# Inverse denominators spread through memory and second-norm statistics on ScalarE, in a fused attention and expert kernel

## What is computed

```
h = layernorm(x) * (1 + ca) + sa
x = x + ga * attention(h)          # 16 heads of 16 channels
h = layernorm(x) * (1 + cb) + sb
x = x + gb * experts(h)            # 1 shared, 8 routed, the best 2 weigh
# attention: q, k scaled and clipped; Tq, Tk Chebyshev orders 1..5
num = sum_n Tq[n] * beta[n] * cumsum(Tk[n] * v)
den = sum_n sum_d(Tq[n]) * beta[n] * cumsum(sum_d(Tk[n]))
out = num / (den + 1e-7)           # den is one number per head and token
# layernorm: (x - mean) / sqrt(var + 1e-5) over the 256 channels
```

## Time and profile before

| what | us |
|---|---|
| median of 3 runs | 1037.01 |
| lowest, highest | 1036.67, 1037.52 |
| the profiled execution | 1036.65 |
| its span in the trace | 1034.9 |

### The profile page before, as it was taken

The page is one execution under the profiler, slowest core; times in us unless marked ns, Lnnn a source line. Parts: engine busy times, 40 slices in busy tenths (PEclk is TensorE's granted clock), DMA queues, the critical chain, the costliest instruction groups (busy, mean ns, idle before and its releaser), DMA issues. The chain is left out here.

```text
span 1034.9 us, 15465 instructions
## 1 busy us (share of the span) xinstructions
PE 935.0 (90%) x4889; PEld 674.1 (65%) x4889; DVE 890.0 (86%) x1385; ACT 475.8 (46%) x702; POOL 399.9 (39%) x631
## 2 busy tenths in 40 slices
PE   3965659999999999999999999999999999989995
PEld 3643346685767676776857676776758676757774
DVE  2488989999999999999999999999999999998431
ACT  4343345553536455554635454455535364431431
POOL 2022454443625244443625253443535152443210
PEclk9977889999999999999999999999999999999998
DMA  8103222223323132223332231232332231312111
GB/s 283 47 1 61 61 41 64 49 63 61 71 45 79 21 63 70 41 61 61 72 61 61 40 69 44 41 73 49 72 61 41 41 72 22 67 36 46 42 21 20
DMA packets 38428, 59.34 MB, mean 57 GB/s; under 512 B 2067, under 2 KB 31198, under 8 KB 38374
## 3 DMA queue, kind: packets, MB, share of 16 engines
q0 software_dynamic: 15360, 33.56, 19.0%
q1 hardware_dynamic: 21410, 22.72, 6.7%
q10 hardware_dynamic: 1604, 2.46, 0.7%
HBM read 16.77 MB, written 16.79 MB: 32 GB/s over the span
## 5 line engine op out<-in xcount | busy, mean ns | idle before, releaser
L797 ACT ACTIVATE hid<-ring,b1row 128x512 f32<-128x512 f32 x144 | 98.6, 685 | 177.5 <-PE ring L1279 177.5
L639 POOL DMA_DIRECT2D feat<-feat x48 | 45.7, 952 | 334.3 <-DVE feat L984 150.3
L1416 PE MATMUL acc<-w,hid 128*128 128x256 f32 x640 | 156.4, 391 | 0.0
L1416 PEld LDWEIGHTS acc<-w,hid 128*128 128x128 f32 x640 | 115.3, 189 | 30.0 <-issue 14.5
L1111 DVE TENSOR_TENSOR hid<-hid,cfb 128x512 f32<-128x512 f32 x128 | 86.3, 674 | 41.8 <-PE cfb L1390 41.1
L752 ACT ACTIVATE feat<-ring,bqkv 128x512 f32<-128x512 f32 x96 | 66.1, 689 | 109.0 <-PE ring L1279 109.0
L963 DVE TENSOR_TENSOR_SCAN feat<-zero,carry,feat 128x512 f32<-128x512 f32 x80 | 111.8, 1446 | 0.0
L963 DVE TENSOR_TENSOR_SCAN feat<-zero,feat 128x512 f32<-128x512 f32 x80 | 108.5, 1403 | 0.0
L1279 PE MATMUL ring<-n2H,w1H 128*128 128x512 f32 x288 | 99.9, 428 | 0.0
L1279 PE MATMUL ring<-n2H,w1L 128*128 128x512 f32 x288 | 91.0, 397 | 0.0
L1279 PE MATMUL ring<-n2L,w1H 128*128 128x512 f32 x288 | 90.6, 395 | 0.0
(11 more groups left out here) (167 smaller groups left out, 2013.9 us busy)
## 6 DMA issues: line engine op xcount, KB each, us to landing
feat<-feat POOLq DMA_DIRECT2D x48, 512.0 KB, 4.6
xin<-in_L_attn_x SPq DMA_DIRECT2D x16, 512.0 KB, 5.4
out<-x SPq DMA_DIRECT2D x16, 512.0 KB, 4.5
out<-fin POOLq DMA_DIRECT2D x16, 512.0 KB, 6.1
gates<-gate_rows SPq DMA_DIRECT2D x16, 128.0 KB, 4.7
feat<-in_L_wmod SPq DMA_DIRECT2D x1, 1536.0 KB, 14.1
feat<-in_L_attn_W_in SPq DMA_DIRECT2D x1, 768.0 KB, 9.5
const<-in_constants ACTq DMA_DIRECT2D x1, 690.5 KB, 4.1
```

Of the source, the lines that this page charges most:

```text
L639: g.dma_start(f(into), f(of), accum_op=ALU.add).then_inc(added[n], 16)
L797: a.activation(hid[:, e % NG], ring[bank][:, :], ACT.Silu, bias=b1row[:, e:e + 1]).then_inc(ring_copied, 1)
L1416: last = mm(acc[t // 2][:, t % 2], x[:, t * P:(t + 1) * P], w[:, e // 2], start=False, stop=(e == E), skip_group_check=True)
```

## The change

The denominators are laid out anew: eight products accumulate in one PSUM tile of 128 rows (head times 8 plus block of 64 tokens) by 64 columns, so `invert` works on 128x64. `spread_inverse` leaves TensorE; SP writes the inverses to device memory and reads them back with each head's row repeated for its 16 channels, into the buffer `attn`, and `divide` multiplies in place. The selection matrix `headsel` is gone from the constants.

The second norm's statistics leave VectorE. ScalarE sums each token's channels (`token_sums`), GpSimd makes the negated mean (`token_means`), ScalarE sums the squared differences (`token_squares`, in two halves), and GpSimd makes scale and shift in four instructions (`inv_std_of_squares`). The passes stand between the copies of the projections; `scale_even` moves behind `normalise_second`. SP's loop is unrolled. VectorE's product for order 3 also waits for the squares, since their output is scratch in its buffer.

```diff
-        denom = sb("denom", [P, 2, P])
+        denom = sb("denom", [P, 2, TB])          # TB = 64, NB = 8
+        inv_rows = nc.dram_tensor("inv_rows", [H, CT], f32).ap()
+        squared = feat[:, W + 2].rearrange("p h (a d) -> p (h a) d", a=NT // KD)
...
+        def token_sums(act, i, p):
+            c = number(i, p)
+            for t in range(NT):
+                act.wait_ge(x1_ready, 2 * c + 1 + t // 2)
+                last = nc.scalar.activation(squared[:, t], x1[:, p, t], ACT.Copy, accum_out=ms[:, 1, 0, t:t + 1])
+            last.then_inc(sums_ready, 1)
+        def token_means(pool, i, p):
+            pool.wait_ge(sums_ready, number(i, p) + 1)
+            nc.gpsimd.tensor_tensor(ms[:, 1, 1], ms[:, 1, 0], k_("-1/D", NT), ALU.mult).then_inc(mean_ready, 1)
+        def token_squares(act, i, p, half):
+            act.wait_ge(mean_ready, number(i, p) + 1)
+            for t in (2 * half, 2 * half + 1):
+                last = nc.scalar.activation(squared[:, t], x1[:, p, t], ACT.Square, bias=ms[:, 1, 1, t:t + 1],
+                                            accum_out=ms[:, 1, 2, t:t + 1])
+            last.then_inc(squares_ready, 1)
+        def inv_std_of_squares(pool, i, p):
+            pool.wait_ge(squares_ready, 2 * c + 2)
+            # mult by 1/D; add eps; pow -half; mult by the negated mean, each behind the one before
...
 # SP
+            def spread_inverse(i, p):
+                c = number(i, p)
+                sp.wait_ge(den_inv, c + 1)
+                sp.dma_start(inv_rows.rearrange("h (b t) -> (h b) t", b=NB), denom[:, 1]).then_inc(inv_written, 16)
+                sp.wait_ge(added[0], 16 * (c + 1))
+                sp.wait_ge(inv_written, 16 * (c + 1))
+                for k in range(KD):
+                    rows = inv_rows[k * HPH:(k + 1) * HPH].unsqueeze(1).to_broadcast([HPH, DH, CT])
+                    sp.dma_start(attn[:, k], rows).then_inc(inv_spread, 16)
                 if loads or i < B:
+                    spread_inverse(i, p)
                     store_x1(i, p)
-            with sp.Fori(2, B - 2) as i:
+            for i in range(2, B - 2):
...
 # GpSimd
-                    inv_std(pool, 1, *later(i, p, -1))
+                    token_means(pool, *later(i, p, -1))
+                    inv_std_of_squares(pool, *later(i, p, -1))
...
 # ScalarE
                     highs(0, *nxt)
+                if second:
+                    token_sums(act, *prev)
                 silu(2)
-                if attn_:
-                    scale_even(i, p)
-                for half in HALVES[:4]:
-                    copy(half)
+                copy("k0")
+                if second:
+                    token_squares(act, *prev, 0)
+                copy("k1")
+                if second:
+                    token_squares(act, *prev, 1)
+                copy("q0")
+                copy("q1")
                 if second:
                     normalise_second(act, *prev)
+                if attn_:
+                    scale_even(i, p)
                 silu(3)
...
 # VectorE
                     dve.wait_ge(odd_ready, 4 * c + 1)
+                    ge(dve, squares_ready, 2 * c)
...
-                v.tensor_scalar(denom[:, 0], misc[:, 0:P], EPS_DEN, None, ALU.add).then_inc(den_eps, 1)
+                v.tensor_scalar(denom[:, 0], misc[:, 0:TB], EPS_DEN, None, ALU.add).then_inc(den_eps, 1)
...
+                dve.wait_ge(inv_spread, 32 * (c + 1))
                 for k in range(KD):
-                    dve.wait_ge(inv_spread, 2 * c + k + 1)
-                    v.tensor_tensor(attn[:, k], feat[:, W, k], tr[k][:, :], ALU.mult).then_inc(attn_ready, 1)
+                    v.tensor_tensor(attn[:, k], feat[:, W, k], attn[:, k], ALU.mult).then_inc(attn_ready, 1)
...
                     residual(*prev)
-                    token_stats(dve, 1, *prev)
...
 # TensorE
-                for t in range(NT):
-                    last = mm(misc[t * QS:(t + 1) * QS, 0:P], cv["densum"],
-                              prod[:, t * P:(t + 1) * P], start=True, stop=True)
+                for b in range(NB):
+                    last = mm(misc[:, 0:TB], cv["densum"][:, b * P:(b + 1) * P],
+                              prod[:, b * TB:(b + 1) * TB], start=(b == 0), stop=(b == NB - 1))
...
                 expert(5)
-                if attn_:
-                    spread_inverse(i, p)
                 expert(6)
```

More of the change, by code:

```diff
@@ L27 @@
 LQ = 2 * QS
+NB = P // H
+TB = CT // NB
 XS = 4
@@ L54 @@
 ROWS = head_rows()
-CONSTS = {"ident": P, "headsum": 4 * QS, "densum": QS, "headsel": NT * KD * P, "kshift": 1, "rowmask": 2,
+CONSTS = {"ident": P, "headsum": 4 * QS, "densum": NB * P, "kshift": 1, "rowmask": 2,
           "biases": 2, "tie": E * E, "cfsel": E * P}
@@ L71, in constants @@
             w = GAMMA[n] if n in (0, 2, 4) else 1.0
-            for copy in range(QS // H):
-                c["densum"][row, copy * H + half * HPH + h] = w
+            for b in range(NB):
+                c["densum"][row, b * P + (half * HPH + h) * NB + b] = w
             c["kshift"][row, 0] = {1: -0.5 * DH, 3: -0.125 * DH}.get(n, 0.0)
-    for q in range(4):
-        for half in range(KD):
-            c["headsel"][q * QS + half * HPH + ch // DH, (q * KD + half) * P + ch] = 1.0
     c["rowmask"][:SPL // 2, 0] = 1.0
@@ L113, in build @@
         tie = cv["tie"].unsqueeze(1).to_broadcast([P, NT, E * E])
-        PC = ("-half", "half", "one", "eps", "1/D", "e")
+        PC = ("-half", "half", "one", "eps", "1/D", "-1/D", "e")
         pool_c = sb("pool_c", [P, len(PC)])
@@ L227, in build @@
         rstd_ready = [sem(f"rstd{n}_ready") for n in range(2)]
+        sums_ready, mean_ready = sem("token_sums"), sem("token_means")
+        squares_ready, var_steps = sem("token_squares"), sem("token_variance_steps")
         norm_ready = [sem(f"normalised{n}") for n in range(2)]
@@ L247, in build @@
         den_ready, den_eps, den_inv = sem("denominators"), sem("denominators_eps"), sem("denominators_inverse")
-        inv_spread = sem("inverse_spread")
+        inv_written, inv_spread = sem("inverse_written"), sem("inverse_spread")
         attn_ready = sem("attention_ready")
@@ L376, in token_stats @@
             last.then_inc(stats_ready[n], 1)
+        def token_sums(act, i, p):
[15 more added lines that the diff above has]
+            c = number(i, p)
+            at = 3 * c
+            t = lambda k: ms[:, 1, k]
+            pool.wait_ge(squares_ready, 2 * c + 2)
+            nc.gpsimd.tensor_tensor(t(3), t(2), k_("1/D", NT), ALU.mult).then_inc(var_steps, 1)
+            pool.wait_ge(var_steps, at + 1)
+            nc.gpsimd.tensor_tensor(t(4), t(3), k_("eps", NT), ALU.add).then_inc(var_steps, 1)
+            pool.wait_ge(var_steps, at + 2)
+            nc.gpsimd.tensor_tensor(t(9), t(4), k_("-half", NT), ALU.pow).then_inc(var_steps, 1)
+            pool.wait_ge(var_steps, at + 3)
+            nc.gpsimd.tensor_tensor(t(11), t(1), t(9), ALU.mult).then_inc(rstd_ready[1], 1)
         def normalise_first(act, i, p):
@@ L435, in _ @@
                 for n, what in enumerate(PC):
-                    value = {"-half": -0.5, "half": 0.5, "one": 1.0, "eps": EPS_LN, "1/D": 1.0 / D, "e": math.e}[what]
+                    value = {"-half": -0.5, "half": 0.5, "one": 1.0, "eps": EPS_LN, "1/D": 1.0 / D, "-1/D": -1.0 / D, "e": math.e}[what]
                     nc.gpsimd.memset(pool_c[:, n:n + 1], value).then_inc(s_pow, 1)
@@ L845, in step @@
                     highs(0, *nxt)
+                if second:
+                    token_sums(act, *prev)
                 silu(2)
+                copy("k0")
[6 more added lines that the diff above has]
+                copy("q1")
+                if second:
+                    normalise_second(act, *prev)
                 if attn_:
                     scale_even(i, p)
-                for half in HALVES[:4]:
-                    copy(half)
-                if second:
-                    normalise_second(act, *prev)
                 silu(3)
```

## The result

The change makes the kernel slower: 1059.5 us in the median of four runs (1055.11 to 1064.64) against 1037.26 of before (1036.67 to 1038.57), a ratio of 1.0215 (95% interval 1.0186 to 1.0244). The profiled execution took 1060.72 us, its span is 1058.9 against 1034.9.

What follows compares the result with a forecast made beforehand. It took TensorE and VectorE to share the lead, each in one half of a step. Thirteen steps at +1.2 us gave +15.6, the ends +1; on 1036.65 that made 1053 us, own range 1042 to 1068, wider range 1030 to 1075.

Steps and rivals of the forecast that it cites:

- the steady loss: Per full step +1.6 +0.1 -0.5 = +1.2 us, over thirteen full steps +15.6 us.
- the ends: First and last steps, where less work covers the chains: +1 us for both together.
- Halves: TensorE leads about 38 us from expert 7 to the next step's expert 4, VectorE the other 19.5 us.
- VectorE's removed bn_stats: Four calls, 1.40 us a step, in the half TensorE leads: their removal was costed at nothing.
- Inversion: `invert` at half width, in the half VectorE leads: 0.5 us a step gained.
- Denominators on TensorE: Sixteen instructions, 1.9 us in all, in the half VectorE leads: nothing on the path.
- ScalarE's chain: Sums, squares and moved `scale_even` up to expert 2's `hidden_high` make TensorE's products 1.6 us late a step.
- the moved stall: GpSimd's `weigh_order_5` moves a 2.1 us VectorE stall to a later scan: 0.1 us a step on average.
- Transfers: Inverses by memory land 6.4 us after the reciprocal, hidden ahead of `divide`: 0 us a step exposed.
- The rival of exposed transfers: Repeated-row reads take 7.5 us, `project_out` is 1.4 us late, times 15: +20, so 1073 us; chance 0.19.

Runs made afterwards that it cites:

- first_stats_moved: The kernel before, with only the first norm's bn_stats on VectorE moved ahead of the multiply of expert 2; 1033.4 us, ratio 0.9953.
- half_inverted: The kernel before, with `invert` working on only the first 64 of its 128 columns; 1032.3 us, ratio 0.9943.
- scale_even_back: The change, with `scale_even` put back behind `silu(2)`, ahead of the copies on ScalarE; 1056.7 us, ratio 1.0170.
- transfers_only: The change's inverses by memory alone, with the second norm's statistics and the orders as in the kernel before; 1047.8 us, ratio 1.0093.
- gpsimd_early: The change with `scale_even` back behind `silu(2)`, and `weigh_order_5` and `scale_wo` ahead of the second norm's instructions on GpSimd; 1054.0 us, ratio 1.0185.

## Why the prediction was right, and where its terms were not

Direction and size were right: 1053 forecast with 1042 to 1068 as the forecast's own range, 1059.5 measured. That the number came so near is in part luck: the steady loss was forecast too high and the ends too low. The inside of the sum, by its own steps:

- **Halves.** The split at expert 4 and expert 7 held. VectorE's removed bn_stats were worth nothing, as costed: after the change it idles 2.54 us where it used to work, and TensorE's half is not a bit shorter. `first_stats_moved` is the counter-test: the same 1.3 us in the other half give 1.35.
- **Inversion.** 0.5 us forecast, 0.46 measured (0.22 + 0.55 for 0.28 + 0.95), and by `half_inverted` it accounts for the gain of the second part, all but the 0.2 us that came with the statistics.
- **Denominators on TensorE.** 1.9 us forecast, 1.99 measured for the sixteen instructions, off the path.
- **ScalarE's chain.** 1.7 us late forecast (with GpSimd's 0.1), 1.19 measured. The place was right (`hidden_low` of expert 2), and so was that `scale_even` behind the normalise costs time by itself (0.5 forecast, 0.4 measured). What was mis-sized is the price of an instruction with a sum: 0.40 us for a copy and 0.49 for a square from start to start, where I took 0.55 and 0.62. The read of the sum is an instruction of its own, 0.19 us, of which 0.1 shows. So both lie near the forecast's lower bound of 0.417, and the normalise was 0.4 us late in steps with `scale_wo` and 0.8 in the others, not 1.1. And ScalarE's chain is what TensorE waits for in the steps without `scale_wo` only.
- **GpSimd.** I charged 0.1 for the moved stall. With ScalarE mended it costs 1.2 us in steps with `scale_wo` and 0.5 in the others, as `scale_even_back` shows (26.36 and 25.65 for 25.12). In the change the stalled scans end 0.5 us behind ScalarE's high part in the first kind and hide behind it in the second. So this term was mis-sized: two delays of like size stood side by side, and I counted one.
- **Transfers.** Steady: hidden, as forecast. The write landed in 1.4 us (1.5 taken), both reads 6.1 us after the reciprocal (6.4 taken), and in steps 2 to 15 `divide` waits once, 0.4 us. The rival of exposed transfers fell for these, not by its premise but by its price. The Trainium skill's rule ("DMA: Bandwidth & Descriptors", section on why a semaphore rises by 16) would put these reads on 8 of 16 engines. The trace agrees: in step 8 the DMA engines are busy to 0.51 while the reads run, and eight of their packets are under way at once more often than any other number. But from issue to landing both together took 4.6 us, the 4.5 I had taken, and not 7.5.
- **The ends.** This is the term that failed: +1 us forecast for both ends, +14 measured (10.6 without step 2, which the forecast counted as a full step). I said that less work covers the chains there and did not work it out. In step 0 VectorE reaches `divide` 5.6 us behind the reciprocal, which the timeline of before would have told, so that even the 6.4 us of the forecast would not have been covered; the chain took 10.4 us, the first write alone 4.5, beside GpSimd's transfer. TensorE waits 12.6 us for it, and the granted clock is at its lower level from 86.5 to 107.0: the change has 72 us at the lower clock before 250 us, the kernel before 48. By third `project_out`, the statistics alone cost 4.1 us of the 12.05 and the early transfers 5.6. The remaining 2.3 belong to neither alone, and the trace has their place: behind a gap of 1.73 us at expert 6 of step 2 the clock falls at 212.8 for 6.8 us (windows of 3 us), and that step's second part takes 35.25 us. In `transfers_only` and `gpsimd_early`, where the clock holds there, it takes 32.2.

```profile
209.00:212.00 3.00, 1.27 (x8) 0.74 (x7) 2.91 (x5) 2.67 (x6) 0.54 (x1) 1.00 0.18 68
...
215.00:218.00 3.00, 3.00 (x9) 2.37 (x8) 1.70 (x3) 1.00 (x1) 2.44 (x6) 0.50 0.00 0
```

- **The clock.** The sum has no term for it. The forecast counted what TensorE's work and waits would be, and not what a gap does to the work behind it.

So from step 3 on a loss of 10 us, and a start and end of 14; by the forecast's own thirteen steps, 2 to 14, it is 13.4 where 15.6 was forecast, and 10.6 at the ends where 1 was: two errors of opposite sign. The 10 us are some 0.6 in each full step, one clock fall worth 1.3, and 1.5 in step 15, which has two clock falls of 3.4 us, at 936.4 and 960.3, where before has one.

**Open.** What makes the clock fall behind one gap and not behind the next. In steps 2 to 13 of `transfers_only` it fell behind all five gaps of 1.94 us at expert 6 and behind three of the seven of 1.63 to 1.75 us; in the change, where all twelve gaps are of 1.62 to 1.76 us, it fell behind two. The filling shows that the gap is a condition, and its length seems to count; what decides beyond that, no run here tells apart.

## What to carry to other kernels

When two engines share the lead, ask in which part of the step each leads before pricing a removed instruction: here 1.3 us of VectorE were worth nothing in one half and 1.35 us in the other, and moving work between the halves gained, though the first part gave 0.4 or 1.2 us of it back. Of an instruction that is moved, ask what stands right behind its new place on its engine, not only who waits for its result. And work out the first and last iterations on their own, since a latency that the steady state hides is bare there. Look at the gaps of TensorE too: a change that joins two short ones can cost more than it takes away.

## What was not expected of the hardware

- Moving work from between two gaps of TensorE (1.11 and 0.73 us) to ahead of them made a step 0.6 us longer in `transfers_only`: behind the one gap of 1.65 or 1.94 us the granted clock went to its lower level for 3.4 us in eight of twelve steps, and filling the gap with products of constants took 7.6 us off the kernel.
- A sum on ScalarE over 256 columns shows as an ACTIVATE of 0.41 us and an ACTIVATION_READ_ACCUMULATOR of 0.19 to 0.20 us that start 0.30 us apart; the pair repeats every 0.40 us for a copy and every 0.49 us for a square with its bias.
- Two GpSimd multiplies in SBUF stretched two VectorE scans from 2.33 to 4.27 us; the first of them had begun before the scans. One alone stretched two scans from 2.45 to 3.6 us.
- A write of 32 KB landed after 4.5 us beside a 512 KB transfer that filled the DMA engines; the median of all sixteen is 1.4.
- Two reads of 256 KB whose source has 8 rows as its slowest dimension kept the DMA engines busy to 0.51, and still landed together 4.6 us after their issue.
